# The second tile's probabilities turned in four pieces, and the sums and splits of the ffn matrix one step later, in a fused cross-attention and ffn kernel on one core

## The reference

```python
xn = layernorm(x)                                  # x: 4 x 2048 x 512, f32
q, k, v = xn @ Wq, context @ Wk, context @ Wv      # 16 heads of 64; 77 keys a batch
attn = softmax(q k^T / 8)
x = x + tanh(g_xattn) * ((attn v) @ Wo + bo)
idx = argmax(log_softmax(logits) + gumbel(u))      # picks one of 8 ffn matrices
x = x + tanh(g_ffn) * (layernorm(x) @ W[idx] + b[idx])
```

## Time and profile before

| | |
|---|---|
| median of 3 runs | 1055.47 us (1053.39 to 1059.3) |
| the profiled execution | 1055.75 us, its span 1054.0 us |
| PE busy | 1037.3 us, 98% of the span |
| DVE busy | 847.1 us, 80% |
| ACT busy | 742.5 us, 70% |
| POOL busy | 436.9 us, 41% |
| chain of work that ended last, PE's share | 91% |
| turns of the DMA queue | 258, median 3.0 us to landing |

### The profile page before, as it was taken

One profiled execution on the slowest core, in us unless ns is written; L12 is line 12 of the kernel. 1 busy time (PEld: TensorE's weight loads), 2 busy tenths in 40 slices (PEclk: granted clock), 3 DMA queues, 4 the chain that ended last, 5 costly groups with the idle time before them and its releaser, 6 DMA issues.

```text
span 1054.0 us, 21876 instructions
## 1 busy us (share of the span) xinstructions
PE 1037.3 (98%) x6107; PEld 590.4 (56%) x6107; DVE 847.1 (80%) x1789; ACT 742.5 (70%) x2709; POOL 436.9 (41%) x633
## 2 busy tenths in 40 slices
PE   8998899999999999999999999999999999999998
PEld 6634455555555555555555555555555555555556
DVE  3876988888888887888888887888888887888873
ACT  3587987766776677766776677766776677776770
POOL 0575444444433343444433343444433343444411
PEclk9999999999999999999999999999999999999999
DMA  8423467655566656655576656755576666755564
GB/s 306 101 33 95 97 130 139 133 114 118 128 136 135 135 129 132 139 119 111 126 136 135 135 131 130 140 119 111 124 136 135 135 132 130 141 119 111 123 111 110
DMA packets 381688, 134.38 MB, mean 128 GB/s; under 512 B 360160, under 2 KB 361236, under 8 KB 381588
## 3 DMA queue, kind: packets, MB, share of 16 engines
q1 hardware_dynamic: 381524, 133.43, 59.4%
q0 software_dynamic: 64, 0.00, 0.0%
HBM read 27.21 MB, written 16.78 MB: 42 GB/s over the span
## 4 chain that ended last, share of the span: by engine, by line
PE 91%; DVE 3%; ACT 3%; DMA 1%; POOL 1%; issue 0%; SPq 0%; DVEq 0%; ACTq 0%
PE banks L1309 83%; PE banks L1525 3%; PE banks L1571 1%; PE banks L1339 1%; PE banks L1348 1%; ACT work L841 1%; PE banks L1412 1%; DMA fold_area<-in_L_xattn_Wv 1%; DVE vw_area L1043 1%; PE banks L1401 1%; DMA work<-work 0%; DVE fold_area L1051 0%; POOL vw_area L635 0%; ACT vw_area L794 0%; DVE work L418 0%
## 5 line engine op out<-in xcount | busy, mean ns | idle before, releaser
L841 ACT ACTIVATE work<-banks,red,cst 128x77 f32<-128x77 f32 x1024 | 410.2, 431 | 87.3 <-DVE red L1134 87.0
L1309 PE MATMUL banks<-fold_area,work 128*128 128x462 f16 (+1 forms) x2304 | 412.1, 337 | 3.1 <-DVE fold_area L1051 2.2
L1309 PE MATMUL banks<-vw_area,work 128*128 128x512 f16 x1674 | 371.4, 379 | 2.5 <-DMA work<-work 2.4
L1309 PEld LDWEIGHTS banks<-fold_area,work 128*128 128x128 f16 x2304 | 224.4, 97 | 179.0 <-issue 4.5
L1309 PEld LDWEIGHTS banks<-vw_area,work 128*128 128x128 f16 x1674 | 163.6, 98 | 187.4 <-DMA work<-work 3.2
L418 DVE SCALAR_TENSOR_TENSOR work<-work 128x256 f16<-128x256 f32 (+3 forms) x444 | 240.2, 575 | 4.3 <-ACT work L864 2.1
L841 ACT ACTIVATION_READ_ACCUMULATOR work<-banks,red,cst 128x1 f32 x1024 | 225.2, 220 | 0.0
L1132 DVE TENSOR_REDUCE stats<-banks 128x6 f32<-128x462 f32 (+1 forms) x192 | 112.1, 584 | 108.7 <-PE banks L1309 108.3
L1309 PE MATMUL banks<-work 128*128 128x256 f16 x1260 | 157.2, 272 | 0.0
L1309 PEld LDWEIGHTS banks<-work 128*128 128x128 f16 x1260 | 122.9, 98 | 30.2
L686 POOL TENSOR_TENSOR stats<-stats,cst 128x1 f32<-128x1 f32 x64 | 12.3, 192 | 285.9 <-DVE stats L1168 285.9
(11 more groups left out here) (139 smaller groups left out, 824.3 us busy)
## 6 DMA issues: line engine op xcount, KB each, us to landing
work<-in_x SPq DMA_DIRECT2D x64, 256.0 KB, 2.8
out<-work SPq DMA_DIRECT2D x64, 256.0 KB, 2.2
work<-work SPq DMA_TRANSPOSE x258, 3.0
fold_area<-in_L_xattn_Wo SPq DMA_DIRECT2D x4, 512.0 KB, 9.4
work<-in_L_ffn_W SPq DMA_DIRECT2D x2, 1024.0 KB, 7.0
fold_area<-in_L_xattn_Wq SPq DMA_DIRECT2D x2, 1024.0 KB, 12.9
fold_area<-in_L_xattn_Wk SPq DMA_DIRECT2D x2, 768.0 KB, 12.3
fold_area<-in_L_xattn_Wv SPq DMA_DIRECT2D x2, 384.0 KB, 6.8
```

Of the source, the lines that this page charges most:

```text
L841: nc.scalar.activation(probs_of(h, h + 1), s_bank(m, k)[:, (h - h0) * J:(h - h0 + 1) * J], ACT.Exp, bias=nmx[:, h:h + 1], scale=exp_scale, ...
L1309: mm = nc.tensor.matmul(ps, lhs(l), rhs(r), start=first and n == 0, stop=last and n == 2, skip_group_check=onto)
```

## The change

Four things move, all in steps 0 to 2.

Tile 1 joins `turned_early`: its probabilities go in four turns, each as its part is ready, and PE's attention of tile 1 is written in the four parts. Tile 1 still waits for attention of tile 0 before the first turn, since both use the same place.

`weights_summed` on POOL moves from the end of step 0 to the end of step 1, behind `x_scale` of tile 3. `weights_high` on ACT moves by one step for both lists. `weights_low` on DVE moves by one step as well: `AS_LOADED` from step 1 to step 2, at the same place ahead of `softmax`; `AS_SUMMED` stays in step 2 but goes from that place to behind `probs_low`, ahead of `attention_sum`. The DMA of the ffn bias goes from ahead of tile 1's turn to behind its four turns.

```diff
         def turned_early(o, m):
-            return is_tile(o, m, 0, NT - 1)
+            return is_tile(o, m, 0, 1, NT - 1)
...
-                    elif not early:
+                    elif not early or is_tile(o, m, 1):
                         due(o_done, nth(o, m))
-                    if is_tile(o, m, 1):
-                        sp.dma_start(bias, ffn_b[bass.ds(op, 1), :].to_broadcast([P, D])).then_inc(bias_loaded, 16)
...
                     sp.dma_start_transpose(turned[:, start:, :], ps[:, start * P:]).then_inc(pT_turned, 16)
+                    if is_tile(o, m, 1):
+                        sp.dma_start(bias, ffn_b[bass.ds(op, 1), :].to_broadcast([P, D])).then_inc(bias_loaded, 16)
...
                 pool.wait_ge(wf_again, 16)
-                pool.wait_ge(p_lo, 4)
+                pool.wait_ge(nmx_ready, 2 * len(BANKS))
...
-                if is_tile(o, m, 0):
+                if is_tile(o, m, 1):
                     weights_summed()
...
-                    if is_tile(o, m, 1):
+                    if is_tile(o, m, 1, 2):
                         for part_turned in pT_parts:
-                            act.wait_ge(part_turned, 16)
+                            act.wait_ge(part_turned, 16 * number(o, m))
...
-                if is_tile(o, m, 0):
+                if is_tile(o, m, 1):
                     weights_high(AS_LOADED)
-                if is_tile(o, m, 1):
+                if is_tile(o, m, 2):
                     weights_high(AS_SUMMED)
...
-                if is_tile(o, m, 1):
+                if is_tile(o, m, 2):
                     weights_low(AS_LOADED, 0)
-                if is_tile(o, m, 2):
-                    weights_low(AS_SUMMED, len(AS_LOADED))
...
                     probs_low(o, m, 0)
                     probs_low(o, m, 1)
+                if is_tile(o, m, 2):
+                    weights_low(AS_SUMMED, len(AS_LOADED))
...
-                turns = 16 if is_tile(o, m, 0) else 32
+                turns = 16 if is_tile(o, m, 0) else 32 if is_tile(o, m, 1) else 48
```

## The result

The change is slower: 1064.12 us median of 5 runs (1061.12 to 1066.38) against 1055.49 us (1053.39 to 1059.3); the ratio is 1.0067, 95% interval 1.0047 to 1.0087. The profiled execution has a span of 1064.6 us, 10.6 more than before.

The account below looks back on a forecast made before the run. PE bound the kernel, busy 1037.3 of 1054.0 us, so at most 3.6 us could be won. New DVE and POOL delays made attention of tile 3 3.9 us late, taken as +3.8: a median of 1059.3, range 1053.8 to 1061.4.

Parts of the forecast that it names:

- Both waits of before: PE's waits before scores of tile 2 (0.90 us) and attention of tile 1 (2.40 us), both forecast to go.
- the sums on POOL made L1179 wait: DVE's L1179 of tile 0 was to wait for POOL until 123.0, 2.2 us late.
- the three splits lost a microsecond to L710: DVE's splits ahead of softmax of tile 2: 2.05 us, plus 1.25 us blocked by POOL's addition L710.
- the four splits held `attention_sum` of tile 1: On DVE, the AS_SUMMED splits were to hold it 2.73 us, to 135.0, 4.85 us late.
- attention of tile 3 can start 5.2 us later: PE's start on tile 3 was put 5.2 us behind attention_sum at 147.85, a distance read at tile 2.
- the forecast of 153.05: Forecast start of PE's attention of tile 3, which began at 149.17 before: +3.9 us.
- `attention_sum` after it begins 10.43 us on: DVE's attention_sum was to follow the first exponential of tile 3 by 10.43 us, at 147.85.
- The clock: The new 2.9 us wait may halve PE's clock for scores of tile 3: nothing, or up to 1 us.
- rival E: Experiments' rival: the late start belongs to the changed program; scores of tile 0 at 91.0 before, 95.3 changed; no chance given.
- D: Experiments' theory: the first context load lands late by chance, up to some 4 us, in either kernel.
- The third rival: Splits and POOL's additions block each other more than once, or the clock falls twice: +6.3 us, 1061.8; 14%.
- in this stretch it and ACT set the pace: From 105.8 to 127 us, gapless DVE was read as setting the pace with ACT, not PE.

Follow-up runs that it names:

- e3: The change with the sums on POOL back in step 0; ratio to the kernel before 1.0052 [1.0032, 1.0073].
- e12: The change with the AS_LOADED splits back in step 1 (ACT's in step 0); ratio to the kernel before 1.0046 [1.0030, 1.0063].
- e5: The change with the ffn bias fetched ahead of tile 1's four turns; ratio to the kernel before 1.0069 [1.0054, 1.0085].
- e6: The kernel before with only tile 1's four turns added, the bias still ahead of them; ratio 1.0003 [0.9989, 1.0018].
- e9: The kernel before, unchanged, run and profiled once more; ratio 1.0007 [0.9994, 1.0021].
- e4: The change itself, run and profiled once more; ratio to the kernel before 1.0079 [1.0060, 1.0098].
- e1: The kernel before with only the moves of sums and splits, without tile 1's four turns; ratio 1.0084 [1.0065, 1.0103].
- e7: e6 with the four AS_SUMMED splits on DVE moved behind probs_low of tile 2; ratio to the kernel before 1.0063 [1.0044, 1.0081].
- e10: e6 with tile 2 in four turns as well; ratio to the kernel before 1.0019 [1.0005, 1.0034].

## Why the prediction was wrong

**What held.** Both waits of before went, and attention of tile 1 began at 118.9 on the old axis (119.1); the sums on POOL made L1179 wait, to the tenth; `x_low` of tile 3 came late by what stands ahead of it, and PE waited 2.8 us (2.9); the three splits lost a microsecond to L710 (3.08 against 2.07 us); attention of tile 2 was at 137.0 on the old axis (137.5); the four splits held `attention_sum` of tile 1 (134.6 against 135.0). e3 and e12 show the two parts one by one: late sums 3.7 us, late `AS_LOADED` 2.2 us at attention of tile 3, each with the other present. The ffn bias cost nothing (e5).

**The step that failed** is "attention of tile 3 can start 5.2 us later". It took 7.03 us (159.82 - 152.79), and that is 1.8 of the 2.3 us by which the forecast of 153.05 missed 155.35. I had taken the distance from tile 2's turn, 5.20, as if turns were alike. Tile 3's turn took 5.5 us already before, and ended 0.4 us ahead of its use; in the change it took 6.8. In thirteen profiles it is a single turn: in ten a code load began well inside it and it took 6.6 to 7.0 us, in three (before, e6, e9) it took 5.5 and the load began in its last 0.12 us or behind it. With the pairs above, in one kernel, the load is the likely cause; no kernel was run in which only the load moves.

**A second term was too small**: "`attention_sum` after it begins 10.43 us on". From the first exponential of tile 3, at 141.51, to 152.79 it was 11.28, with the 4.90 us to the reciprocal as forecast and the rest in the two operations of DVE beside POOL's L704 and L710 that are shown above, 3.33 instead of 2.34 us. As `attention_sum` of tile 1 was 0.4 us earlier than forecast, 0.5 is left of it at that of tile 2.

**The clock** was a term I costed at "nothing, or up to 1 us", for the wait ahead of scores of tile 3. There it was so: in e4 scores of tile 3 took 8.11 instead of 6.43, and the next wait took it up, 0.63 instead of 2.51 us. But I looked at that wait alone. The longest, 3.8 us, stands ahead of attention of tile 3, and nothing behind it takes anything up: 1.7 us in e4, e1 and e5. The Trainium skill's warning about waits between bursts ("TensorE: Matmul & The Clock Gate", section "Why this matters for your kernels") agrees, though not in each execution: the first profile of the change was granted 1.00 there.

**The start.** Of the profile's 10.6 us, 4.35 lie ahead of the changed stage. I had left such a spread out of the range altogether. It is there in the runs of one program (t0 95.3 and 92.5), but no more than that can be said: three of the 14 profiles start above 95, all of them with moved sums or splits, yet four others of that kind start at 90.4 to 92.9. e9, the kernel before once more, started at 91.2, which is what rival E had said and D allows.

So 3.9 forecast, 0.5 and 1.8 more, up to 1.7 by the clock make 6.2 to 7.9 us in the stage. The loss is 8.6 us by the medians and 7.1 by the ratio; what the stage leaves of it may lie in the start, which added 4.5 and 1.7 us in the two profiles of the change, but the other executions were not profiled. The third rival, "clearly slower" by 6.3, came nearest in size, and its mechanism was right in part: more operations were blocked, for 0.9 us, and the clock fell in one of the two profiles, but the largest piece, the late landing, is not in it.

**One reading was wrong without hurting the sum:** in "in this stretch it and ACT set the pace", the "it" (DVE) fails for `softmax` of tile 2, which waited for ACT. e7 shows that DVE's row had no gap only because the splits filled one.

## What to carry to other kernels

A gapless engine is not the one that sets the pace: ask for each operation whether the next one would have started sooner without it. Work that fills another engine's wait is free, and the same work a few operations later, behind the wait, costs its full time; one such line, with what it set off, cost as much as this whole change. When a transfer ends within half a microsecond of its use, all that makes it later must be priced with what else it can then meet, and more than one wait must be checked for the clock.

## What the runs showed of the hardware

A DMA turn of 20 blocks in which a load on q8 (the profile's "instruction" kind, one packet of 0.02 MB) began 3.1 to 4.7 us after the issue took 6.6 to 7.0 us in ten profiles, and 5.5 in the three in which the load came at its end or later; the same instruction of the loop took 6.5 to 6.6 us with such a load and 4.8 to 4.9 without. In the change 8 to 9 GB/s moved for 1.2 us of it. A load in about a turn's first microsecond went with no longer time (4.4 to 5.0 us).

In one and the same program PE waited 3.24 us for a load of the context in one execution and 0.95 in another. A 256 KB broadcast load issued behind four turns landed after 3.2 to 5.1 us in five profiles, and after 3.1 to 3.4 in the nine in which it was issued ahead of tile 1's turn or turns.

After waits of 3.6 to 3.9 us at one place, PE's granted clock fell to 0.50 in four profiles (e1, e4, e5, e7) and stayed at 1.00 in three (the change, e3, e10).
